# A larger pump credit for an interleaved scan, smaller weight loads, and two moves between engines, in a Mamba-attention-MoE layer on eight cores

## What is computed

```python
xn    = ln(y)
delta = sigmoid(xn @ Wdelta + bdelta)          # 16 wide
Bt    = xn @ Win + b_in                        # 16 wide
gate  = sigmoid(xn @ Wgate + bgate)
def step(h, inp):                              # 4096 times, one after the other
    d_t, B_t = inp
    h = tanh(h * d_t @ A + B_t)                # A is 16 x 16
    return h, h
mamba = h_all @ C * gate + y
q, k, v = (ln1(y) @ W + b for W in (Wq, Wk, Wv))   # 8 heads of 128
x2    = y + softmax(q k^T / sqrt(128)) v @ Wo + bo
t_out = x2 + relu(ln2(x2) @ W1 + b1) @ W2 + b2     # 1024 -> 4096 -> 1024
out1  = x + lnf(concat(mamba, t_out) @ Wf + bf)
y2    = ln(out1)
out   = out1 + top-2-of-8 SwiGLU experts(y2) + mean of 2 shared SwiGLU experts(y2)
```

## Time and profile before

| | us |
|---|---|
| three runs | 9257.54, 8653.28, 8484.24 |
| median | 8653.28 |
| the profiled execution | 8489.35 |
| its span on the slowest core (core 0) | 8487.5 |
| spans of the eight cores | 8443.0 to 8487.5 |

### The profile page before, as it was taken

One profiled execution on the slowest core, in us unless ns is written; L12 is line 12 of the kernel. 1 busy time (PEld: TensorE's weight loads), 2 busy tenths in 40 slices (PEclk: granted clock), 3 DMA queues, 4 the chain that ended last, 5 costly groups with the idle time before them and its releaser, 6 DMA issues.

```text
span 8487.5 us, 94373 instructions; the slowest of 8 cores (8443.0 to 8487.5 us)
## 1 busy us (share of the span) xinstructions
PE 6205.6 (73%) x30774; PEld 2697.5 (32%) x31320; DVE 2297.9 (27%) x4269; ACT 2536.9 (30%) x6186; POOL 243.4 (3%) x295
## 2 busy tenths in 40 slices
PE   3446747667475558478223369999999799999999
PEld 1213314233141122122111134444444344444444
DVE  3332131221313344344343312222222222222221
ACT  3545547466463333233231121111111111111111
POOL 0000000000000000000000000000000000000000
PEclk6666768767686679789556689999999999999999
DMA  2110120201102222212113263544344444354442
GB/s 62 45 57 13 38 52 18 65 14 43 43 21 82 72 56 47 66 34 40 56 50 91 73 111 64 86 70 80 60 79 76 104 78 72 60 84 76 70 70 60
DMA packets 464597, 517.18 MB, mean 61 GB/s; under 512 B 112370, under 2 KB 382962, under 8 KB 464130
## 3 DMA queue, kind: packets, MB, share of 16 engines
q0 software_dynamic: 252256, 304.27, 22.1%
q1 hardware_dynamic: 211874, 206.84, 8.0%
HBM read 756.60 MB, written 54.53 MB: 96 GB/s over the span
## 4 chain that ended last, share of the span: by engine, by line
PE 67%; ACT 9%; DVE 9%; issue 7%; DMA 5%; SPq 1%; DVEq 0%; ACTq 0%; POOLq 0%
PE psA L1598 13%; PE psB L1611 13%; PE ps5a L1650 7%; PE ps5b L1650 7%; ACT halls L522 4%; PE psS L518 4%; DVE ascs L497 2%; ACT expbs L903 2%; PE ps5b L1198 2%; PE psA L1226 1%; PE psB L1226 1%; PE psA L888 1%; PE ps5a L919 1%; PE ps5a L1198 1%; DMA xb<-x_own 1%
## 5 line engine op out<-in xcount | busy, mean ns | idle before, releaser
L522 ACT ACTIVATE halls<-psS,btTs 16x1 bf16<-16x1 f32 x4096 | 1028.7, 251 | 2112.9 <-PE psS L518 2105.0
L518 PE MATMUL psS<-halls,ascs 16*16 16x1 bf16 x4095 | 661.7, 162 | 1279.7 <-ACT halls L522 1102.6
L1598 PE MATMUL psA<-y2hs,w1es 128*128 128x512 bf16 x4994 | 1202.3, 380 | 113.4 <-DMA y2hs<-y2T_d 106.0
L1611 PE MATMUL psB<-y2hs,w2es 128*128 128x512 bf16 x5036 | 1203.3, 379 | 4.3
L518 PEld LDWEIGHTS psS<-halls,ascs 16*16 16x16 bf16 x4095 | 333.1, 81 | 2388.7 <-issue 2348.9
L1624 ACT ACTIVATE s1bs<-psA,rb1cs 128x512 bf16<-128x512 f32 x512 | 351.8, 687 | 2372.0 <-PE psA L1598 2302.8
L1633 DVE SCALAR_TENSOR_TENSOR glubs<-psB,rb2cs,s1bs 128x512 bf16<-128x512 f32 x512 | 384.4, 751 | 1430.3 <-PE psB L1611 1347.1
L1598 PEld LDWEIGHTS psA<-y2hs,w1es 128*128 128x128 bf16 x5120 | 498.9, 98 | 708.8 <-issue 115.2
L1611 PEld LDWEIGHTS psB<-y2hs,w2es 128*128 128x128 bf16 x5120 | 501.5, 98 | 606.1 <-issue 3.5
L1650 PE MATMUL ps5a<-w3es,glubs 128*128 128x512 bf16 x2508 | 575.2, 379 | 27.6 <-DVE glubs L1633 23.6
L1650 PE MATMUL ps5b<-w3es,glubs 128*128 128x512 bf16 x2506 | 575.1, 380 | 4.3 <-issue 2.2
(11 more groups left out here) (274 smaller groups left out, 5527.5 us busy)
## 6 DMA issues: line engine op xcount, KB each, us to landing
w1es<-rw POOLq DMA_DIRECT2D x64, 1024.0 KB, 8.3
w2es<-rw POOLq DMA_DIRECT2D x64, 1024.0 KB, 11.8
w3es<-rw POOLq DMA_DIRECT2D x16, 4096.0 KB, 26.7
ytg<-ytT_d SPq DMA_DIRECT2D x48, 512.0 KB, 3.4
xb<-x_own SPq DMA_DIRECT2D x48, 512.0 KB, 4.4
ytg<-ytT_d SPq DMA_DIRECT2D x20, 1024.0 KB, 5.4
ytg2b<-ytT_d SPq DMA_DIRECT2D x20, 1024.0 KB, 5.4
xbigs<-x_full SPq DMA_DIRECT2D x32, 512.0 KB, 8.1
```

Of the source, the lines that this page charges most:

```text
L518: A("tensor", lambda e, ring=ring, off=off, hp=hprev: e.matmul(psS[0:16, 0:1], ring[:, off:off + 16], hp, start=True, stop=True), reads=[r ...
L522: A("scalar", lambda e, t=t: e.activation(hall[:, t:t + 1], psS[0:16, 0:1], AF.Tanh, bias=btT[:, t:t + 1]), reads=[PSC, f"btT{t // 512}"], ...
L1598: e.matmul(psA[:, po:po + 512], w1e[wb][:, c * 512 + mc * 128: c * 512 + (mc + 1) * 128], y2h[:, c * 1024 + tg * 512: c * 1024 + (tg + 1) ...
L1611: e.matmul(psB[:, po:po + 512], w2e[wb][:, c * 512 + mc * 128: c * 512 + (mc + 1) * 128], y2h[:, c * 1024 + tg * 512: c * 1024 + (tg + 1) ...
```

## The change

Six edits, none of which changes what is computed:

1. The credits of VectorE and ScalarE operations go up: 900 to 1200, 1500 to 2000, 500 to 600, 400 to 500, 300 to 400, 800 to 900, and 260 to 380 where the tag isn't listed.
2. Where the target is 600, each DMA adds 300; up to three steps are emitted at once, not two.
3. The loads of x in p1 go from the SP queue to the POOL queue.
4. W1 of the feed-forward is loaded in four quarters per chunk, not two halves, with a key each.
5. `w1e` and `w2e` of the experts are loaded in two halves each, with a key each, in the order w1 half 0, w2 half 0, w1 half 1, w2 half 1.
6. In the mamba output the cast (mocast) and the two evictions of the transposes go from ScalarE to VectorE.

```diff
-        VS_COST = dict(lng_sq=900, lng_sum=900, yhat=900, x2h=900, fnorm=900,
-                       y2h=900, fg=900, fbias=900, o1=900, gsel0=1500,
...
+        VS_COST = dict(lng_sq=1200, lng_sum=1200, yhat=1200, x2h=1200,
+                       fnorm=1200, y2h=1200, fg=1200, fbias=1200, o1=1200,
+                       gsel0=2000, gsel1=2000, p4y=1200, bmy=1200, fev=600,
+                       tr8ev=600, xn2ev=600, exp=900, kev=500, vev=400,
+                       qev=500, xnT=600, xn1T=600, qxn=600, gxn=600,
+                       relu=500, momul=600, moadd=1200, mocast=600,
+                       ln_sq=1200, ln_sum=1200)
...
-                scan_state["credit"] += VS_COST.get(tag, 260)
+                scan_state["credit"] += VS_COST.get(tag, 380)
+            elif dma and scan_state["target"] <= 600.0:
+                scan_state["credit"] += 300
...
-                n = min(int(scan_state["credit"] // scan_state["target"]), 2)
+                n = min(int(scan_state["credit"] // scan_state["target"]), 3)
...
         def p1_load_ln(g):
...
-                dma("sync", xbig[:, j * 1024:(j + 1) * 1024],
+                dma("gpsimd", xbig[:, j * 1024:(j + 1) * 1024],
...
-                for hf in range(2):
+                for hf in range(4):
                     dma("gpsimd",
-                        w1c[fb][:, hf * 2048:(hf + 1) * 2048].rearrange(
-                            "p (c f) -> p c f", c=4),
...
+                        w1c[fb][:, hf * 1024:(hf + 1) * 1024].rearrange(
+                            "p (c f) -> p c f", c=2),
...
-                              reads=[f"{w1k}_h{c // 4}", "xn2T", pk],
+                              reads=[f"{w1k}_q{c // 2}", "xn2T", pk],
...
-            A("scalar", lambda e, b_=bsel: e.activation(
-                ybf[b_][:], mob[:], AF.Identity),
+            A("vector", lambda e, b_=bsel: e.tensor_copy(ybf[b_][:], mob[:]),
...
-                       "tstage", banks=TRB3, evac="scalar")
+                       "tstage", banks=TRB3)
...
+                    for kf in range(2):
+                        dma("gpsimd",
+                            w1e[wb][:, kf * 2048:(kf + 1) * 2048].rearrange(
+                                "p (c f) -> p c f", c=4),
...
+                            [f"w1e{wb}_h{kf}"], [f"w1e{wb}_h{kf}"],
+                            tag="w1e")
+                        dma("gpsimd",
+                            w2e[wb][:, kf * 2048:(kf + 1) * 2048].rearrange(
+                                "p (c f) -> p c f", c=4),
...
-                                         f"y2h{tg * 4 + 3}", w1k, pka],
+                                         f"y2h{tg * 4 + 3}",
+                                         f"{w1k}_h{c // 4}", pka],
```

More of the change, by code:

```diff
@@ L1562, in build_nc @@
                     wb = hc % 2
[L1563 to L1567, removed]
-                        wsrc2.ap()[eidx][:, hc * 512:(hc + 1) * 512]
-                        .rearrange("(c p) f -> p c f", p=128),
-                        [f"w2e{wb}"], [f"w2e{wb}"], tag="w2e")
+                    for kf in range(2):
+                        dma("gpsimd",
+                            w1e[wb][:, kf * 2048:(kf + 1) * 2048].rearrange(
+                                "p (c f) -> p c f", c=4),
+                            wsrc1.ap()[eidx][kf * 512:(kf + 1) * 512,
+                                             hc * 512:(hc + 1) * 512]
+                            .rearrange("(c p) f -> p c f", p=128),
+                            [f"w1e{wb}_h{kf}"], [f"w1e{wb}_h{kf}"],
[3 more added lines that the diff above has]
+                                "p (c f) -> p c f", c=4),
+                            wsrc2.ap()[eidx][kf * 512:(kf + 1) * 512,
+                                             hc * 512:(hc + 1) * 512]
+                            .rearrange("(c p) f -> p c f", p=128),
+                            [f"w2e{wb}_h{kf}"], [f"w2e{wb}_h{kf}"],
+                            tag="w2e")
                 dma("gpsimd", w3e[:].rearrange("p (c f) -> p c f", c=16),
@@ L1579, in build_nc @@
                     if hc >= 2:
-                        dma("gpsimd", w1e[wb][:].rearrange("p (c f) -> p c f", c=8),
-                            wsrc1.ap()[eidx][:, hc * 512:(hc + 1) * 512]
-                            .rearrange("(c p) f -> p c f", p=128),
-                            [w1k], [w1k], tag="w1e")
-                        dma("gpsimd", w2e[wb][:].rearrange("p (c f) -> p c f", c=8),
-                            wsrc2.ap()[eidx][:, hc * 512:(hc + 1) * 512]
-                            .rearrange("(c p) f -> p c f", p=128),
-                            [w2k], [w2k], tag="w2e")
+                        for kf in range(2):
+                            dma("gpsimd",
+                                w1e[wb][:, kf * 2048:(kf + 1) * 2048]
+                                .rearrange("p (c f) -> p c f", c=4),
+                                wsrc1.ap()[eidx][kf * 512:(kf + 1) * 512,
+                                                 hc * 512:(hc + 1) * 512]
+                                .rearrange("(c p) f -> p c f", p=128),
+                                [f"{w1k}_h{kf}"], [f"{w1k}_h{kf}"],
+                                tag="w1e")
+                            dma("gpsimd",
+                                w2e[wb][:, kf * 2048:(kf + 1) * 2048]
+                                .rearrange("p (c f) -> p c f", c=4),
+                                wsrc2.ap()[eidx][kf * 512:(kf + 1) * 512,
+                                                 hc * 512:(hc + 1) * 512]
+                                .rearrange("(c p) f -> p c f", p=128),
+                                [f"{w2k}_h{kf}"], [f"{w2k}_h{kf}"],
+                                tag="w2e")
                     for mc in range(4):
@@ L1618, in build_nc @@
                                          f"y2h{tg * 4 + 2}",
-                                         f"y2h{tg * 4 + 3}", w2k, pkb],
+                                         f"y2h{tg * 4 + 3}",
+                                         f"{w2k}_h{c // 4}", pkb],
                                   writes=[pkb], tag="p2mm")
```

9 lines of the change are left out of this document (2 added, 7 removed).

## The result

The changed kernel took 8742.35 us (median of 10 runs) and the kernel before, run beside it, 8572.37 us (median of 10). In some executions the cores of one die or of both run at a lower clock for much of the time, whichever kernel it is; these executions, and such cores of a profile, are left out of every comparison here, which leaves one to three executions of most experiments. The ratio is 1.0295, 95% interval 1.0281 to 1.0308: slower. The profiled execution took 8748.05 us, its slowest core is core 3 (span 8746.2). That is 258.7 us above the profiled execution of before, where 179 were forecast. The median, 8742, and this 8748 lie within the range given (8560 to 8760) and are 2 and 8 us beyond the one that stood beside the forecast (8600 to 8740).

The account below looks back on a forecast made before the run. TensorE was taken as the bound, with steps priced by their place. Paid 262 us (p4a 76 the largest) less 83 saved gave 8489 + 179 = 8668 us, ratio 1.021; forecast 8600 to 8740, range 8560 to 8760.

Parts of the forecast that it names:

- upper bound: Whole kernel: all 545 moved steps cost 0.65 us and the later start 24, less 83 saved: +295, 8784 us.
- rival 2: Whole kernel: every added step is bare, with no matmuls between steps emitted together; 8784 us, chance 0.12.
- p4a: Stage p4a: 141 added steps, some 120 of them bare between the last gate and first Wo matmul; +76 us.
- saving in the second feed-forward: Second feed-forward: 245 steps leave it, 4.55 of its chunks become bare; 302 us against 362, say 58 saved.
- the first feed-forward at 24: First feed-forward: 57 added steps, 20 from five DMAs per chunk, the rest at 0.25 us or a little more; +24 us.
- Rival 4: Feed-forward without steps: the clock rises to full from 0.94, at most 10 us; chance 0.04 together with others.
- mostly hidden: Q parts: 52 added steps, mostly covered by other work; +6 us.
- x on POOL: Start of p1: first x waits behind the weights on POOL's queue; 18 us later, between 15 and 24.
- The mamba output: Mamba output: cast and evictions on VectorE and one step round fewer save 1.4 us a tile, 22 us; stage near 335.
- Smaller loads: W1 in the feed-forward and the experts' weights: same bytes in smaller loads; cost 0, with 10 us either way.
- rival 3: Experts: smaller loads matter, at most half of the 106 us of y2h waits is gained; 8615 us, chance 0.06.
- Rival 1: Whole kernel: added steps lie under other waits at 0.07 us each; -27, 8462 us, not slower; chance 0.12.

Follow-up runs that it names:

- after_no_dma_credit: The changed kernel without the 300 of credit that each DMA adds; 8704.7 and 8710.0 us, beside 8494.9 to 8502.1 for the kernel before.
- after_ffn_even: The changed kernel with feed-forward credit from TensorE's matmuls alone (305.2 each), same step count, evenly spread; 8692.3 us, beside 8497.4 to 8502.3 for the kernel before.
- rest_only: The changed kernel with the old credits, so edits 3 to 6 alone; ratio 0.9988 to the kernel before, interval 0.9966 to 1.0009.
- p4a_credits_only: The kernel before with the new credits (DMA credit included, two steps at once) in p4a alone; lowest run 8568.3 us, +76.

## Why the prediction was right and wrong

**The direction and the mechanism held.** The edit only exchanges places, from the covered ones at the end to uncovered ones earlier. The count of steps in each stage came out as worked out: 691 by the end of p1 (696), 228 in the second feed-forward, none after it. One total in the prediction is wrong: what the second feed-forward, the last output part and the mamba output give up is 245 + 29 + 324 = 598 steps, and not 545, which leaves out the 57 of the first feed-forward. The stage-by-stage sum doesn't use it; the upper bound and rival 2 do, and are 8821 us with it, not 8784.

**Prices that held**: bare steps at 0.655 in the statistics parts (+47.1 for +42), the bound parts (+26.1 for +28), p1 (+66.9 for +62), p4a at equal clock (+76.2 for +76). The saving in the second feed-forward was 53.0 where 58 were forecast, again at a clock that varied: core 3 had it at 320.5 us, core 0 at 308.6. In p4a the sum is right and its parts are partly luck: the prediction had the DMAs' steps, two a tile, among the bare ones, and by after_no_dma_credit they cost next to nothing (0.03) and those of the raised costs more than a bare step (0.73).

**The term that was mis-sized most**: the first feed-forward at 24. The step that failed is the price: "20 of its 57 steps come from five DMAs in a row per chunk, bare but for the first (1.3 us a chunk), the rest at 0.25 or a little more". The 0.25 came from the earlier trace rows, where seven steps lie among 16 matmuls; it is the average over the distances of before (118 us over 472 steps) and no constant: more steps in the same matmuls push each other closer, and so make dearer the steps that were there already. The run with the same steps spread shows it, 4.3 us of waiting against 40.1. The 57 steps are worth 37 us instead of 24, that is 0.65 each, with the clock left out.

**The term that was set to nothing**: the clock. Rival 4 let it rise in a feed-forward without steps, and no term let it fall where steps were added. The first feed-forward had 8.6 us of it. The three K and V parts hold the same operations and got the same number of steps more, and grew by 25, 11 and 6 us. The first of them, that of the second head group, has 25.4 us of the 42.1: on core 0 its granted clock fell from 0.76 to 0.63, and TensorE was busy for 105.85 us where it had been for 89.63, with 22 more steps that make 3.5 of those 16; TensorE's waits for the tanh grew there by 7.9 us (43.7 to 51.6). Without the credit of the DMAs, with 7 steps fewer, the same part was back at a clock of 0.75 and 149 us with a build in it, no more than the 139 without one before; there it is the last of the three parts that grew, by 15 us. So the size of this loss doesn't follow from the number of steps. In the Q parts 57.25 us of busy time became 67.15 in one and less in the others; beside it the steps in Q were not "mostly hidden": 52 of them brought 22.8 us. The prediction took their cover from the shape of the stage and not from a row of waits, and that is the step that failed there.

What makes the clock fall is open. It is not the stops for matrices: with these gone that K and V part still took 162.7 us in the changed kernel, as with them (176.3 less 12.6). It differs between cores that run the same program. The first feed-forward of after_ffn_even on core 0 and then on core 7, the same instructions:

```profile
3364.60:3756.50 391.90, 350.39 (x1569) 105.12 (x1569) 159.28 (x223) 134.63 (x529) 28.49 (x40) 0.96 0.27 44
```
```profile
3361.70:3774.50 412.80, 372.30 (x1569) 106.28 (x1569) 159.24 (x223) 134.61 (x530) 28.56 (x40) 0.89 0.28 42
```

21 us between them, with the clock at 0.96 and 0.89. The metric takes the slowest of eight, and so a forecast from one core's rows has such a stage's luck in it.

**x on POOL.** The forecast was 18 us later, first used near 33, and 12.6 of it given back in the groups after (1.8 in each of seven). Timeline of core 0:

```profile
20.71 2.17 POOL L307 DMA_DIRECT2D xbigs<-x_full  x4
...
32.17 1.22 DVE L421 TENSOR_SCALAR_CACHE_REDUCE dmp2b<-xbigs 128x1024 bf16<-128x1024 f32 x1 [19.86 <-DMA xbigs<-x_full]
```

32.17 against 15.09, 17 later, behind Wv in the queue. In rest_only x is first used at 33.92, 18.8 later, and p1 is 1.1 us longer in all: the earlier loads give back nearly everything, so the move cost 1 us and not 5.

**The mamba output**: near 335 was said for the stage, 323.9 came, as one build had left it too. The 335 had forgotten that the build of 12.6 us leaves the stage with its steps; less the build 16.8 were saved and not 22. The 22 were 0.8 a tile for edit 6, 13 in all, and 0.6 a tile for the step that falls away, 10 in all: by rest_only edit 6 gave 6.6, and the other 10.2 came with the steps gone. A tile's tail now (core 0):

```profile
4494.84 0.69 DVE L1339 CAST ybf<-mobs 128x1024 bf16<-128x1024 f32 x1
...
4498.00 0.37 SPq L307 DMA_DIRECT2D moT_d<-tstage  x1
...
4502.69 1.22 DVE L381 SCALAR_TENSOR_TENSOR dmpb<-xb 128x1024 bf16<-128x1024 f32 x1 [4.77 <-DMA xb<-x_own]
```

From moadd's end (4494.74) to the store it is 3.3 us, 3.8 before and 3.0 in the sum; the load behind the store still sets the pace.

**Smaller loads.** Nothing, as forecast. The whole trace's waits for matrices and for y2h in core 0 of the changed kernel, beside the earlier trace rows:

```profile
PE psS L520 <- DVE ascs L499: 155.1, 12, 19.7
PE psA L1617 <- DMA y2hs<-y2T_d: 106.3, 3, 43.4
```

106.3 us after 106.0: rival 3 fell, and the experts took 3607.3 us where they had taken 3604.2 (means).

**The rivals.** Rival 1 fell with p4a_credits_only: 0.52 a step, far over 0.12. Rival 2, every added step bare, is nearer than its chance of 0.12 allowed: the stages that grew, less the start, paid about 320 us for the 598 moved steps, 0.54 each, in the middle between the 0.41 of the sum (262 - 18 over 598) and its own 0.65. In the first feed-forward its price came true, 0.65 at equal clock, but not its reason: only 31 of the steps became bare. Rival 4 was too small to see: the second feed-forward ran at 0.98 on core 0, where it had 0.94, and the clock took more than that back in the stages before.

## What to carry to other kernels

The price of an operation slipped into another engine's stream depends on its distance to the one before, when the two are links of one chain: here 0.66, 0.44, 0.22 and 0.19 us with none, one, two and three matmuls of 512 columns between. So place the links by that engine's own work and not by a credit from other engines or DMAs; that alone was worth 50 us with the count unchanged. And before moving links of a chain earlier, look for places in which something else ends last (here a load, at 0.04 us a step for 20 steps a tile and 0.12 for those beyond) and leave them there; then take out the stops of the chain itself, which at 138 us were worth more than any placing tried here.

## What the runs showed of the hardware

- The round of a 16x16 matmul, a tanh on 16x1 and back is 0.655 us, and it stays so with one or two 512-column matmuls (0.216 us each) between: with two, the round costs 0.22 us beyond them.
- The granted clock of the same instructions differs by core: 0.89 and 0.96 over the same 400 us stage, 21 us apart, with neither a difference in waits nor in DMA traffic beside it (0.27 and 0.28 of the DMA engines' time).
- Taking work away from a mixed stage lowered its clock: with 133 fewer steps in p4a 390 of its 512-column matmuls ran at the lower level, 235 with them; in the first feed-forward without builds and without waits for the tanh four cores had 5 to 10 of them at that level, and the other four some 89.
- Four loads of x behind the weights on POOL's queue were used 11.5 us after their issue (20.71 to 32.17), on SP 4.7 us after (10.36 to 15.09).
